# An LSTM with residual: the stationary and the moving operand of the recurrence change places

## The reference

```python
xW = jnp.einsum('ntd,dk->tnk', x, Wx) + b
def step(carry, xw_t):
    prev_h, prev_c = carry
    a = xw_t + prev_h @ Wh
    i = sigmoid(a[:, 0:H]); f = sigmoid(a[:, H:2*H]); o = sigmoid(a[:, 2*H:3*H]); g = tanh(a[:, 3*H:4*H])
    next_c = f * prev_c + i * g
    next_h = o * tanh(next_c)
    return (next_h, next_c), next_h
_, hs = scan(step, (cond, 0), xW)
return x + transpose(hs, (1, 0, 2))
```

## Time and profile before

| what | value |
|---|---|
| median of 3 runs | 1101.32 us (1098.41 to 1105.87) |
| the profiled execution | 1104.56 us, span of instructions 1102.8 us |
| mean granted TensorE clock | 0.962 |
| TensorE matmuls | busy 701.9 us, 64% of the span, 36864 records |
| TensorE weight loads | busy 578.7 us, 52%, 36864 records |
| VectorE | busy 790.9 us, 72% |
| ScalarE | busy 550.2 us, 50% |
| GpSimd | 0.7 us |
| chain that ended last, by engine | DVE 50%, PE 25%, ACT 14%, issue 8%, DMA 2% |
| chain that ended last, by line | L295 38%, L363 25%, L313 8%, L211 8%, L214 6% |
| instruction DMA, all engines | q8: 9 packets, 0.15 MB; q14: 4 packets, 0.03 MB |

### The profile page before, as it was taken

How to read it: one execution, slowest core, us unless ns; L and a number is a source line. 1 busy time by engine, 2 the same in 40 slices (tenths; PEclk the granted TensorE clock), 3 DMA queues, 4 the chain that set the end, 5 groups by cost and what they waited for, 6 DMA issues and landing times.

```text
span 1102.8 us, 88125 instructions
## 1 busy us (share of the span) xinstructions
PE 701.9 (64%) x36864; PEld 578.7 (52%) x36864; DVE 790.9 (72%) x4897; ACT 550.2 (50%) x3586; POOL 0.7 (0%) x6
## 2 busy tenths in 40 slices
PE   1766666666666666666666666666666666666664
PEld 1555555555555555545555555555555555555554
DVE  2676777777777767777767777777777777777776
ACT  0454555545555545555545555555555555455544
POOL 0000000000000000000000000000000000000000
PEclk9998999989999989999989999999999999899989
DMA  2000000000000000000000000000000000000000
GB/s 85 6 6 6 5 7 6 6 6 6 6 6 6 6 6 5 6 7 6 6 7 5 6 6 6 6 6 6 6 6 5 7 6 6 6 6 6 6 6 7
DMA packets 31869, 8.73 MB, mean 8 GB/s; under 512 B 31344, under 2 KB 31344, under 8 KB 31856
## 3 DMA queue, kind: packets, MB, share of 16 engines
q1 hardware_dynamic: 31248, 8.41, 3.2%
q10 hardware_dynamic: 608, 0.14, 0.1%
HBM read 6.43 MB, written 2.10 MB: 8 GB/s over the span
## 4 chain that ended last, share of the span: by engine, by line
DVE 50%; PE 25%; ACT 14%; issue 8%; DMA 2%; DVEq 1%; SPq 0%
DVE turned_bank L295 38%; PE gates L363 25%; DVE h_pad L313 8%; ACT tanh_o L211 8%; ACT turned_bank L214 6%; DVE scan_both L300 3%; DMA wh_raw<-in_L_cond_Wh_dram 2%; DVEq L329 1%; DVE cell L306 1%; DVE h_rows L269 0%; SPq L142 0%; SPq L137 0%; DVEq L268 0%; DVE wh L224 0%; DVE wh L221 0%
## 5 line engine op out<-in xcount | busy, mean ns | idle before, releaser
L363 PE MATMUL gates<-wh,h_pad 128*32 128x64 f32 x32768 | 594.7, 227 | 374.8 <-DVE h_pad L313 371.0
L363 PEld LDWEIGHTS gates<-wh,h_pad 128*32 128x32 f32 x32768 | 509.8, 114 | 489.1 <-DVE h_pad L313 485.1
L295 DVE STREAM_TRANSPOSE turned_bank<-gates 128x64 f32<-128x64 f32 x2048 | 478.5, 262 | 184.0 <-PE gates L363 170.8
L202 ACT ACTIVATE tanh_f<-turned_bank 128x8 f32<-128x8 f32 x512 | 90.7, 177 | 449.1 <-DVE turned_bank L295 417.5
L209 ACT ACTIVATE scan_both<-turned_bank 128x8 f32<-128x8 f32 x1024 | 185.1, 181 | 61.1 <-DVE turned_bank L295 19.7
L313 DVE SCALAR_TENSOR_TENSOR h_pad<-tanh_o,turned_bank 128x4 f32<-128x4 f32 x1024 | 132.8, 158 | 74.4 <-ACT turned_bank L214 5.2
L306 DVE TENSOR_TENSOR_SCAN cell<-scan_both 128x12 f32<-128x12 f32 x1024 | 143.8, 181 | 1.9 <-issue 0.3
L214 ACT ACTIVATE turned_bank<-cell 128x4 f32<-128x4 f32 x1024 | 143.3, 172 | 2.3 <-DVE cell L306 0.3
L345 PE MATMUL x_acc<-wx,x_units 128*32 128x128 f32 x2048 | 108.8, 287 | 16.6 <-DVE x_units L248 16.6
L211 ACT ACTIVATE tanh_o<-turned_bank 128x8 f32<-128x8 f32 x512 | 90.7, 177 | 29.2 <-DVE turned_bank L295 7.0
L215 ACT ACTIVATE half_d<-cell 128x8 f32<-128x8 f32 x512 | 100.4, 196 | 0.0
(11 more groups left out here) (24 smaller groups left out, 6.7 us busy)
## 6 DMA issues: line engine op xcount, KB each, us to landing
x_next<-in_x_dram SPq DMA_DIRECT2D x256, 8.0 KB
x_here<-in_x_dram SPq DMA_DIRECT2D x256, 8.0 KB
out_dram<-y_rows SPq DMA_DIRECT2D x256, 8.0 KB
wx_raw<-in_L_cond_Wx_dram SPq DMA_DIRECT2D x2, 512.0 KB
wh_raw<-in_L_cond_Wh_dram SPq DMA_DIRECT2D x2, 512.0 KB
bias_raw<-in_L_cond_b_dram ACTq DMA_DIRECT2D x4, 32.0 KB, 3.5
h_rows<-in_cond_dram ACTq DMA_DIRECT2D x4, 1.0 KB
```

The source lines that it names most:

```text
L202: nc.scalar.activation(tanh_f[:], of_step(BF, t), ACT.Tanh).then_inc(tanh_f_done, 1)
L295: nc.vector.transpose(turned[k], gates[k][:, 0:W]).then_inc(gates_turned[k], 1)
L363: last = nc.tensor.matmul(gates[k][q * R:(q + 1) * R, 0:W], h_stationary(b, t), wh[:, b, q, columns_of(k)], start=False, stop=b == M - 1, ...
```

## The change

The weights become stationary and h moves. A product of the recurrence has a 128x32 piece of Wh as stationary operand and the 4 columns of h of one row block (`h_units[:, b, (t - 1) % STEPS, :]`) as moving operand, and lands with units on partitions and the 4 sequences on columns. A bank has two parts, for instance G and I of half 0, so `recur(b, k)` is 8 products and a step has 64. ScalarE reads the gates from the PSUM banks as they are; the four turns a step are gone. The order of banks and of h's halves is as before. tanh of the cell goes to SBUF.

There are two sets of four gate banks. A set takes 4 steps (SET = 4, 16 columns a part). `x_part(k, s)` fills bank k of set s for four steps at once: for each of 2 parts 4 products of the bias row with ones and 8 of Wx with 16 columns of x, 24 products. One x_part follows each step's O bank: after steps 0 to 3 for set 1 of this chunk, after steps 4 to 7 for set 0 of the next. The bank x_acc, the inject, the addition L234, the identity and the permuted copies of the weights go. The weights are scaled where they lie. VectorE's transpose of the next x moves from t = 2 to t = 4 and waits for x_used, which TensorE raises after the x_part of step 3. The loops stay as they are.

```diff
+    SET = STEPS // 2
+    SETS = STEPS // SET
+    SC = SET * N
...
+    PARTS = (((F, 0), (F, 1)), ((G, 0), (I, 0)), ((G, 1), (I, 1)), ((O, 0), (O, 1)))
...
+        h_units = sb("h_units", [128, M, STEPS, N])
...
-        gates = [ps(f"gates{k}", [128, 512]) for k in BANKS]
-        x_acc = ps("x_acc", [128, 512])
-        turned_bank = [ps(f"turned_bank{k}", [128, 512]) for k in range(3)]
-        turned = [turned_bank[k][:, 0:W] for k in (0, 1, 2)] + [turned_bank[0][:, W:2 * W]]
-        tanh_c = [turned_bank[AB[m]][:, W:W + N] for m in range(M)]
+        gates = [[ps(f"gates{s}{k}", [128, 512]) for k in range(len(PARTS))] for s in range(SETS)]
...
+        def group(t, k):
+
+            at = t % SET * N
+            return gates[t // SET][k][:, 0:2 * SC].rearrange("p (g c) -> p g c", g=2)[:, :, at:at + N]
...
-                    act.wait_ge(gates_turned[BF], now)
-                    nc.scalar.activation(tanh_f[:], of_step(BF, t), ACT.Tanh).then_inc(tanh_f_done, 1)
+                    act.wait_ge(gates_done[BF], now)
+                    nc.scalar.activation(tanh_f[:], group(t, BF), ACT.Tanh).then_inc(tanh_f_done, 1)
...
+            def scale_weights(w, b, factor, loaded):
                 dve.wait_ge(loaded[b], DMA)
-                return permute(made[:, b, :, :], raw[:, b, :].rearrange("p (g q c) -> p g q c", g=NG, q=Q), factor)
-
-            def make_x_part(chunk):
-                dve.wait_ge(x_acc_done, chunk + 1)
-                nc.vector.tensor_tensor(x_part[:], x_acc[:, 0:GC], bias_rows[:], ALU.add).then_inc(x_part_made, 1)
+                if factor != 1.0:
+                    nc.vector.tensor_scalar(w[:, b, G * D:], w[:, b, G * D:], factor, None, ALU.mult)
+                return nc.vector.tensor_scalar(w[:, b, 0:G * D], w[:, b, 0:G * D], 0.5 * factor, None, ALU.mult)
...
-                if ahead and t == 2:
-
+                if ahead and t == SET:
+                    dve.wait_ge(x_used, chunk + 1)
                     dve.wait_ge(x_next_loaded, (chunk + 2) * (Q * DMA))
                     nc.vector.transpose(x_units[:], x_next[:]).then_inc(x_turned, 1)
-                if ahead and t == STEPS - 1:
-                    make_x_part(chunk + 1)
-
-                def turn(k):
-                    dve.wait_ge(gates_done[k], now)
-                    nc.vector.transpose(turned[k], gates[k][:, 0:W]).then_inc(gates_turned[k], 1)
...
-                turn(BF)
-                turn(BA)
-                turn(BB)
                 forget()
-                turn(BO)
                 update(0)
                 update(1)
...
-            def x_product(b, columns, chunk):
-
-                opens = (b, columns) == PIECES[0]
-                if opens:
-                    pe.wait_ge(x_turned, chunk + 1)
-                for q in range(Q):
-                    last = nc.tensor.matmul(x_acc[q * R:(q + 1) * R, columns], x_units[:, b * R:(b + 1) * R],
-                                            wx[:, b, q, columns], start=opens, stop=b == M - 1,
-                                            tile_position=(0, q * R), skip_group_check=True)
-                if (b, columns) == PIECES[-1]:
-                    last.then_inc(x_acc_done, 1)
-
-            def inject(k):
-
-                for q in range(Q):
-                    nc.tensor.matmul(gates[k][q * R:(q + 1) * R, 0:W], ident[:, q * R:(q + 1) * R],
-                                     x_part[:, columns_of(k)], start=True, stop=False,
-                                     tile_position=(0, q * R), skip_group_check=True)
+            def weights(w, b, gate, m, q):
+                at = gate * D + q * QD + m * R
+                return w[:, b, at:at + R]
+
+            def x_part(k, s):
+
+                for g, (gate, m) in enumerate(PARTS[k]):
+                    where = slice(g * SC, (g + 1) * SC)
+                    for q in range(Q):
+                        at = gate * D + q * QD + m * R
+                        nc.tensor.matmul(gates[s][k][q * R:(q + 1) * R, where], bias_row[:, at:at + R], ones[:],
+                                         start=g == 0, stop=False, tile_position=(0, q * R), skip_group_check=True)
+                    for b in range(M):
+                        for q in range(Q):
+                            last = nc.tensor.matmul(gates[s][k][q * R:(q + 1) * R, where], weights(wx, b, gate, m, q),
+                                                    x_units[:, b * R + s * SC:b * R + (s + 1) * SC],
+                                                    start=False, stop=False, tile_position=(0, q * R), skip_group_check=True)
+                return last
             def step(chunk, t, ahead):
                 now = chunk * STEPS + (t + 1)
-                def recur(b, k):
-                    for q in range(Q):
-                        last = nc.tensor.matmul(gates[k][q * R:(q + 1) * R, 0:W], h_stationary(b, t),
-                                                wh[:, b, q, columns_of(k)], start=False, stop=b == M - 1,
-                                                tile_position=(0, q * R), skip_group_check=True)
+                def recur(b, k, parts=(0, 1)):
+                    for g in parts:
+                        gate, m = PARTS[k][g]
+                        for q in range(Q):
+                            last = nc.tensor.matmul(group(t, k)[q * R:(q + 1) * R, g, :], weights(wh, b, gate, m, q),
+                                                    h_units[:, b, (t - 1) % STEPS, :], start=False, stop=b == M - 1,
+                                                    tile_position=(0, q * R), skip_group_check=True)
                     return last
                 pe.wait_ge(h_done[0], now)
                 recur(0, BF)
                 pe.wait_ge(h_done[1], now)
                 recur(1, BF).then_inc(gates_done[BF], 1)
-                for k in (BA, BB, BO):
-                    recur(0, k)
-                    recur(1, k).then_inc(gates_done[k], 1)
-                if t == STEPS - 1 and ahead:
-                    pe.wait_ge(x_part_made, chunk + 2)
-                    for k in BANKS:
-                        pe.wait_ge(gates_turned[k], now)
-                        inject(k)
-                if ahead and 0 <= t - FIRST_PIECE_AT < len(PIECES):
-                    x_product(*PIECES[t - FIRST_PIECE_AT], chunk + 1)
-
+                recur(0, BA)
+                recur(1, BA).then_inc(gates_done[BA], 1)
+                recur(0, BB)
+                recur(1, BB).then_inc(gates_done[BB], 1)
+                recur(0, BO)
+                recur(1, BO).then_inc(gates_done[BO], 1)
+                k, s = t % SET, (t // SET + 1) % SETS
+                if s == 1:
+                    last = x_part(k, 1)
+                    if k == SET - 1:
+                        last.then_inc(x_used, 1)
+                elif ahead:
+                    if k == 0:
+                        pe.wait_ge(x_turned, chunk + 2)
+                    x_part(k, 0)
+
+            pe.wait_ge(bias_made, 1)
+            pe.wait_ge(ones_made, 1)
             pe.wait_ge(wx_made, M)
-            for piece in PIECES:
-                x_product(*piece, 0)
-            pe.wait_ge(ident_made, 1)
-            pe.wait_ge(zeroed, 2)
-            pe.wait_ge(x_part_made, 1)
-            for k in BANKS:
-                inject(k)
+            pe.wait_ge(x_turned, 1)
+            for k in range(len(PARTS)):
+                x_part(k, 0)
             pe.wait_ge(wh_made, M)
             with pe.Fori(0, CHUNKS - 1) as k:
                 for t in range(STEPS):
...
```

More of the change, by code:

```diff
@@ L62, in lstm_residual_kernel @@
         x_here = sb("x_here", [128, QD])
-        x_part = sb("x_part", [128, GC])
         tanh_f = sb("tanh_f", [128, M, N])
         tanh_o = sb("tanh_o", [128, M, N])
+        tanh_c = [sb(f"tanh_c{m}", [128, N]) for m in range(M)]
         half_d = sb("half_d", [128, M, N])
@@ L96, in lstm_residual_kernel @@
         x_turned = sem("x_turned")
+        x_used = sem("x_used")
         x_here_loaded = sem("x_here_loaded")
[L98 to L99 removed]
         h_turned_back = sem("h_turned_back")
@@ L102, in lstm_residual_kernel @@
         y_stored = sem("y_stored")
-        gates_done = [sem(f"gates_done{k}") for k in BANKS]
-        gates_turned = [sem(f"gates_turned{k}") for k in BANKS]
+        gates_done = [sem(f"gates_done{k}") for k in range(len(PARTS))]
         tanh_f_done = sem("tanh_f_done")
@@ L175, in _ @@
         def _(pool):
[L177 to L180, removed]
+            nc.gpsimd.memset(bias_row[:], 0.0).then_inc(bias_zeroed, 1)
+            nc.gpsimd.memset(ones[:], 1.0).then_inc(ones_made, 1)
         @block.scalar
         def _(act):
-            for q in range(Q):
-                act.dma_start(bias_raw[q * R:(q + 1) * R, :, :],
-                              bias.rearrange("(g q c) -> q g c", g=NG, q=Q)[q:q + 1, :, :].broadcast_to(
-                                  [R, NG, QD])).then_inc(bias_loaded, DMA)
             act.wait_ge(zeroed, 1)
@@ L190, in _, with cell_tanh @@
```

(16 more changed lines are left out.)

78 lines of the change are left out of this document (24 added, 54 removed).

## The result

| | before | after |
|---|---|---|
| median of four runs | 1103.59 us | 2990.14 us |
| the profiled execution's span | 1102.8 us | 2997.3 us |
| span / 512 steps | 2.15 us | 5.85 us |

The ratio is 2.710 (95% interval 2.699 to 2.721): slower, as the prediction's sign had it, and far outside its range of 985 to 1480 us.

A forecast was written before the change was run, and what follows sets the result against it. TensorE and VectorE were taken as nearly even before; after the change, TensorE's code fetches bind: 63 turns x 17.8 us + 16 for the last chunk + 32 = 1170 us. Range 985 to 1480 us.

The forecast's parts named there:

- The code of the loop: TensorE's loop body grows to 180 KB, is fetched anew each turn: 17.8 us a turn in place of 15.0.
- I take 1.4, near the low end: transfer plus a third: Time from requesting a 16 KB code block to usable code, taken as 1.4 us; 12 blocks make 16.8 us a turn.
- The bounds of 1.02 and 4.0: Limits in us on a code block's fetch: its packet's transfer from below, on-time steps of the last chunk from above.
- rival 2: A code block takes over 1.8 us to fetch: 1475 us and more (1630 at 2.0); chance 0.12.
- The pace: TensorE's groups of four 128x32 loads follow each other 33 ns apart; 32 groups a step take 1.06 us.
- a few ns a group: What the lower clock was to add to each TensorE group, since loads, not columns, pace it; plus 44 ns of latency.
- rival 1: Code is held or fetched two blocks ahead; steps of 1.87 us, 990 us (908 at the upper clock); chance 0.27.
- 0.30 on faster: Chance that the changed kernel is faster: 0.25 from rival 1 and 0.05 from the forecast of fetched code.
- Rival 3: TensorE's groups pace as with 64 columns, 57 ns: 2.63 us a step, 1379 us, TensorE the bound; chance 0.07.
- The clock: Less streaming in TensorE's array, so 1.2 GHz granted nearly throughout; 990 us there, 908 at the upper clock, code held.
- The end of the step: After O's last record: 0.07 us semaphore to ACT, then 0.55 us from tanh_o to the next first matmul.
- The rule of the Trainium skill on 60 cycles: Each TensorE matmul has some 60 cycles of overhead: 3.2 us a step, near 2050 us; the forecast did not use it.

The follow-up runs named there:

- after_flat: The changed kernel with TensorE's 64 chunks written out, no loop on that engine: 2618.60 us, ratio 2.363 to the kernel before.
- nox_body4_busy: nox_body4 with four idle products of 256 columns behind each O bank, to raise the clock: 1348.95 us, ratio 1.217 to the kernel before.
- nox_body4: The changed kernel without x and bias part, h and gates kept in one place, TensorE's loop body 4 steps (66 KB): 1314.41 us, ratio 1.185 to the kernel before.
- before_bf16: The kernel before with weights, x and h in bfloat16 for TensorE, inject and sums float32: 993.68 us, ratio 0.897.
- after_bf16: The changed kernel with weights, bias, x and h in bfloat16 for TensorE, sums float32: 845.28 us, ratio 0.762 to the kernel before.

## Why the prediction was wrong

- **The code of the loop: right in mechanism, wrong in size.** That 180 KB are not held, that one block ahead is asked for, that 12 blocks and one useless one pass in a turn: 13 packets were measured, and the useless one cost 1.2 us (forecast 1.0). The step that failed is "I take 1.4, near the low end: transfer plus a third". Measured is 3.6 to 3.8 us: the packet's 1.15 (forecast 1.02), 1.2 before it and 1.3 after it. The forecast's own sum with the 3.7 us of straight code, 63 x (12 x 3.7 + 1.0) + 11 x 3.7 for the last chunk + 32, gives 2930 us, 2% short. The bounds of 1.02 and 4.0 held the value; nothing spoke for the low end but that the transfer was the only part with a row. The one row on a DMA's whole latency, 3.5 us from issue to landing, was set aside in rival 2 with 0.12. It lay nearest, though no run shows that the two latencies have the same parts. That the range ended at 1.8 us of a bound of 4.0 was the second fault.
- **What is held.** 99 KB of body were held, 115 KB in every other turn, 131 KB never, and a branch to code not held waited 3.8 us (the kernel after, at 1509.76). The Trainium skill, Runtime: NRT & Kernel Launch, Instruction fetch mechanics, has 128 KB in 16 KB blocks and a wait at such a branch; these runs agree. The same section calls the crossing of a 16 KB boundary mostly hidden; here each costs 3.7 us less what TensorE works off in the meantime, and straight code is no exception (after_flat).
- **The pace: 33 ns was taken, 53 measured.** The guess came out at the upper clock, from which its rows are: 32 ns a group there. What failed is "a few ns a group" for the lower clock, under which the kernel was forecast to run: the difference is 21 ns, 53 at 1.2 GHz. It makes the held step 2.48 us, not 1.87, and rival 1's 990 us false: held, the layout is at 1314 us before any x part. So no price of a block would have made the change faster, and the forecast's sign would have come true without the fetches too. Its 0.30 on faster had no ground. (Rival 1's "1077 if a group takes 40 ns" doesn't follow from its sum either: 31 x 0.040 + 0.85 = 2.09 us a step, 1102 us, no gain.) Rival 3 had this size (1379) with the wrong cause, the columns: x products of 16 columns follow each other 53 ns apart as well, by the starts of single records.
- **The clock** was forecast right, at 1.2 GHz nearly throughout; its effect was not. The profile prints 1.00 for the kernel after because no change of the grant is recorded in it; by 195 ns a record and 53 ns a group, which nox_body4_busy has at a recorded 0.50, the level is 1.2 GHz. A record was forecast at 0.21.
- **The end of the step**, 0.07 + 0.55 us from the end of O's last record on, came out at 0.55 in all: 901.99 to 902.54 in nox_body4. VectorE's turns were on the path, as before_bf16 and after_bf16 show.
- **The rule of the Trainium skill on 60 cycles** (TensorEngine Tiling (Array Packing), Instruction Overhead) gave 25 ns a record, taken at 2.4 GHz; 8 ns were measured at 2.4 GHz and 13 at 1.2, so it asks for two to three times too much here. Its sum came nearer to the result than mine by chance: its cause is not the one found.

What stays open: what the 1.3 us between a packet's end and the first instruction is made of, and why idle products kept the clock up in one layout and not in the other.

## What to carry over

Count the bytes of an engine's code as well as its work: on TensorE a float32 product was 256 bytes, a body up to 99 KB ran free, and from 131 KB on TensorE could pass each 16 KB in no less than about 3.7 us, in a loop or written out. What that costs depends on the work in the block: with 1.7 us of products in 16 KB (the kernel after) over half the time went, with 3.8 us (the kernel before) most of a fetch was hidden and the branch back cost most. A change that doubles the number of products of an engine can so lose far more than it takes off another's path; bfloat16, which halves the bytes and the records alike, turned the same layout from 2.7 times the time into 24% less. Where one part of a latency has a row and the others have none, leave the range open up to the bound.

## What the runs showed of the hardware

A body just over what is held (115 KB) was fetched in every other turn, nine blocks one after another, and free in between. Groups of four 128x32 loads in float32 follow each other 53 ns apart with the clock low, whether 4 or 16 columns move, and 32 ns apart with it high (4 columns); in bfloat16 27 ns apart at best, at a clock that the records don't show. The hint on the branch back saved one of 13 fetches and 4% of the time. A printed granted clock of 1.00 with no recorded change ahead of it went with the pace of 1.2 GHz.
